# Four entry projections of the self attention moved into the end of the cross attention, with shared banks and buffers

## What is computed

```python
x = _layernorm(x + _L0_xattn_ref(x, ctx_1024, mask_BxS2_bf1, ...))   # 16 heads of 128, 8 for k and v
...
attn_out = attention(rmsnorm(hidden_states, norm1_w), wq, wk, wv, wo)  # hidden_states is that x
...
def attention(x, wq, wk, wv, wo):           # H, KV, HD = 16, 4, 128; s = 512
    q = (x @ wq).reshape(b, s, H, HD)
    k = (x @ wk).reshape(b, s, KV, HD)
    v = (x @ wv).reshape(b, s, KV, HD)
    q, k = apply_rope(q, cos, sin), apply_rope(k, cos, sin)
    # scores with a causal mask, softmax over keys, times v, then wo
```

## Time and profile before

| | us |
|---|---|
| median of 3 runs | 1418.55 |
| lowest, highest | 1417.82, 1419.85 |
| the profiled execution | 1419.94 |
| its span | 1418.1 |
| TensorE busy in the span | 1308.9 (92%) |
| VectorE, ScalarE, GpSimd busy | 1023.4, 808.4, 368.7 |
| cross attention's last turn done (XT complete) | 707.4 |
| first matmul of the self attention | 709.99 |
| first scores of the self attention | 727.69 |

### The profile page before, as it was taken

One profiled execution on the slowest core, in us unless ns is written; L12 is line 12 of the kernel. 1 busy time (PEld: TensorE's weight loads), 2 busy tenths in 40 slices (PEclk: granted clock), 3 DMA queues, 4 the chain that ended last, 5 costly groups with the idle time before them and its releaser, 6 DMA issues. The chain is left out here.

```text
span 1418.1 us, 24554 instructions
## 1 busy us (share of the span) xinstructions
PE 1308.9 (92%) x7925; PEld 711.2 (50%) x7925; DVE 1023.4 (72%) x1966; ACT 808.4 (57%) x1460; POOL 368.7 (26%) x602
## 2 busy tenths in 40 slices
PE   7988999999999999999597999999877999999994
PEld 4444444444444444444254555555434556666771
DVE  5847777777777777778668787888778564566676
ACT  5547666666666666667427565565754454455552
POOL 5402020101111110102356465563425100000025
PEclk9999999999999999999799999999988999999997
DMA  8317676667575757598284353535585766677653
GB/s 254 61 36 146 128 134 117 145 119 153 106 155 106 153 108 151 110 180 147 81 256 71 70 142 66 130 65 104 103 164 205 236 232 190 223 240 238 223 149 120
DMA packets 451868, 206.18 MB, mean 145 GB/s; under 512 B 401088, under 2 KB 415424, under 8 KB 451776
## 3 DMA queue, kind: packets, MB, share of 16 engines
q1 hardware_dynamic: 448640, 196.67, 59.2%
q0 software_dynamic: 2560, 8.39, 1.8%
q10 hardware_dynamic: 576, 0.00, 0.0%
HBM read 87.38 MB, written 16.45 MB: 73 GB/s over the span
## 5 line engine op out<-in xcount | busy, mean ns | idle before, releaser
L1546 DVE SCALAR_TENSOR_TENSOR X<-xa_SC,xa_rs,X 128x1024 f16<-128x1024 f32 x128 | 164.4, 1284 | 98.3 <-issue 97.7
L1354 ACT ACTIVATE X<-xa_SC,xa_rs 128x1024 f16<-128x1024 f32 x128 | 147.1, 1149 | 110.4 <-POOL xa_rs L1044 110.4
L1222 PE MATMUL xa_psS<-xa_KT,xa_QT 128*128 128x512 f16 x768 | 186.4, 379 | 6.0 <-DVE xa_mn L1579 4.6
L1234 PE MATMUL xa_psO<-wide,xa_V 128*128 128x512 f16 x768 | 173.5, 383 | 7.5 <-DMA wide<-X 7.5
L1044 POOL TENSOR_SCALAR xa_rs<-xa_rc,flag 128x1 f32<-128x1 f32 x128 | 33.9, 265 | 517.3 <-DVE xa_rc L1539 517.3
L1579 DVE CUSTOM_DVE_ANT_0 xa_SC<-xa_psS,maskb 128x1024 f32<-128x1024 f32 x128 | 155.1, 1212 | 4.7 <-PE xa_psS L1222 2.4
L1376 ACT ACTIVATE xa_SC<-xa_SC,xa_mn 128x1024 f32<-128x1024 f32 x128 | 145.4, 1136 | 13.7 <-DVE xa_mn L1579 13.6
L1234 PEld LDWEIGHTS xa_psO<-wide,xa_V 128*128 128x128 f16 x768 | 74.6, 99 | 102.5 <-issue 17.3
L1222 PEld LDWEIGHTS xa_psS<-xa_KT,xa_QT 128*128 128x128 f16 x768 | 73.4, 98 | 90.6 <-DVE xa_mn L1579 9.4
L1376 ACT ACTIVATE sa_SC<-sa_SC,sa_mn 128x128 f32<-128x128 f32 (+3 forms) x128 | 71.5, 558 | 72.2 <-DVE sa_mn L1579 71.8
L2072 PE MATMUL rmoe_psG<-rmoe_XGT,W 128*128 128x352 f16 (+6 forms) x768 | 108.4, 291 | 2.1 <-DVE rmoe_XGT L2180 2.1
(11 more groups left out here) (295 smaller groups left out, 2253.7 us busy)
## 6 DMA issues: line engine op xcount, KB each, us to landing
first<-in_L_ffn_w_dram SPq DMA_DIRECT2D x12, 2048.0 KB, 12.2
W2raw<-in_L_ffn_w_dram SPq DMA_DIRECT2D x8, 2048.0 KB, 9.2
expert_rows_dram<-zeros SPq DMA_DIRECT2D x10, 512.0 KB, 9.3
xa_WPraw<-in_L_xattn_Wq_dram SPq DMA_DIRECT2D x8, 512.0 KB, 4.8
xa_WOraw<-in_L_xattn_Wo_dram SPq DMA_DIRECT2D x8, 512.0 KB, 4.5
first<-in_L_ffn_wq_dram SPq DMA_DIRECT2D x4, 1024.0 KB, 7.9
first<-in_L_ffn_wo_dram SPq DMA_DIRECT2D x4, 1024.0 KB, 5.8
first<-in_L_ffn_w_dram SPq DMA_DIRECT2D x8, 512.0 KB, 4.9
```

What stands on the lines that cost most here:

```text
L1222: last = nc.tensor.matmul(psS[j % NSC][:, c:c + cw], QT[b][:, hq, g, t * P:(t + 1) * P], KT[b][:, hk, c:c + cw], start=(q == 0), stop=(q = ...
L1234: last = nc.tensor.matmul(psO[:, c:], V[b][:, hv, blk, :], PT[g % NPT][:, blk, hp, c:], start=(blk + q == 0), stop=(blk == NBLK - 1 and q ...
L1354: nc.scalar.activation(PN[j % NPN][:, 0:w // P, 0, :], by_block(SC[j % NSC], w), ACT.Identity, scale=rs[:, j % 4:j % 4 + 1]).then_inc(norm ...
L1546: nc.vector.scalar_tensor_tensor(out=PN[j % NPN][:, 0:w // P, 1, :], in0=by_block(SC[j % NSC], w), scalar=rs[:, j % 4:j % 4 + 1], in1=PN[j ...
```

## The change

- **Where the projections are made.** K, Q0, Q1 and Q2 of batch 0 are made in xa's end by a new `entry_project`, between the turns of batch 1. They need XT of batch 0 complete and the split weights. They go into the banks psO, psJ1, psJ0 and psJ2, which are free once the outputs that were in them have been added.
- **What is done with them there.** VectorE turns K and Q0 (`entry_turn`), GpSimd adds K's two products, ScalarE and GpSimd write K's halves. Q0's sum, and all of Q1 and Q2 after the matmuls, stay for sa, whose engines begin with their semaphores raised by the jobs already made (MADE = 4, TURNED = 2, ROTATED = 1). sa's TensorE begins with Q3 and V, in psO and psJ1.
- **What is shared.** The banks psO and psJ are allocated once for both calls (`banks`). KT0, V0 and the buffers rA and rB lie in the memory of the context CT, which xa no longer reads then (`carried`).
- **Order and waits.** In xa's end VectorE does tile 2's low half before the first output add of batch 1, tile 3's after tile 4's centring, and tile 5's after tile 7's. The second projection in the first head group's steps waits for one job more. The wait for the stores of X stands behind the six jobs on VectorE, not ahead of them.

```diff
 
         if isinstance(h, int) and h == 1 and k < 2:
             return k + 1
+        if causal and isinstance(h, int) and h == 0 and k == 1:
+            return 2
         return 3 if last else (3, 3, 3, 3, 3, 3, 3, 2, 4, 3)[k]
...
+        if causal:
+            KT0, V0, rA, rB = carried
+            QT = [sb(f"QT{b}", [P, 2, groups, S], F16) for b in range(B)]
+            KT = [KT0, sb("KT1", [P, 2, keys], F16)]
+            V = [V0, sb("V1", [P, 2, NBLK, HD], F16)]
+        else:
...
-        rA = [sb(f"rA{i}", [P, S if causal else 1], F32) for i in range(3)]
-        rB = [sb(f"rB{i}", [P, S if causal else 1], F32) for i in range(3)]
...
-        psO = pb("psO", [P, 512])
-        psJ = [pb(f"psJ{i}", [P, 512]) for i in range(NJ)]
-        ring = psJ
+        psO, psJ = banks
         acc = [psS[-1][:, NB * 512 - 512:NB * 512], psJ[1], psJ[0], psJ[2]]
+        entry_bank = [psO, psJ[1], psJ[0], psJ[2], psO, psJ[1]]
+        ring, RING = (entry_bank, 4) if causal else ([psJ[i % NJ] for i in range(JP)], NJ)
+        MADE, TURNED, ROTATED = (4, 2, 1) if causal else (0, 0, 0)
...
+            nK, _, nA, nB = next_carried
...
             if causal:
-                rope_sum(0, 0, 0, 0)
-                for i in range(1, JP - 1):
+                pool.sem_inc(rope_added, ROTATED)
+                pool.sem_inc(rope_done, ROTATED)
+                rope_sum(0, 0, ROTATED, ROTATED)
+                for i in range(ROTATED + 1, JP - 1):
                     rope_sum(0, 0, i, i)
...
+                pool.wait_ge(entry_turned, 1)
+                nc.gpsimd.tensor_tensor(nA[0], nA[0], nB[0], ALU.add).then_inc(entry_added, 1)
+                pool.wait_ge(entry_hi, 1)
+                nc.gpsimd.tensor_tensor(nK[:, 1, :], nA[0], nK[:, 0, :], ALU.subtract).then_inc(entry_lo, 1)
+                pool.wait_ge(entry_lo, 1)
...
                         pe.wait_ge(job_free, jobs_before(h) + t + 1)
                     last_output(t, early)
+
+            def entry_project(i):
+
+                if i == 0:
+                    pe.wait_ge(next_lo, len(next_pieces))
+                    pe.wait_ge(norm_lo, TPB)
+                else:
+                    pe.wait_ge(job_free, last_job(TPB + i) + 1)
+                for q, (hw, hx) in enumerate(PAIRS):
+                    for k in range(DC):
+                        last = nc.tensor.matmul(entry_bank[i][:, :],
+                                                next_k[:, hw, k, :] if i == 0 else next_q[:, hw, k, i - 1, :],
+                                                XT[:, hx, k, 0:S], start=(q + k == 0), stop=(q == 2 and k == DC - 1))
+                last.then_inc(entry_ready, 1)
 
...
+            if MADE:
+                pe.sem_inc(job_ready, MADE)
+            for i in range(MADE, JP):
                 if i == min(i for i, (kind, _) in enumerate(proj) if kind != "q"):
                     wait_from(pe, wp_done, WP0)
-                project(0, 0, i, i, ring[i % len(ring)], len(ring))
...
-                for i in range(TPB, NT):
-                    norm_pe(pe, i)
+                entry_project(0)
+                norm_pe(pe, 4)
+                entry_project(1)
+                norm_pe(pe, 5)
+                norm_pe(pe, 6)
+                entry_project(2)
+                norm_pe(pe, 7)
+                entry_project(3)
...
-            for i in (0, 1, 2, 3, 5, 4) if causal else range(JP):
+            if ROTATED:
+                act.sem_inc(rope_hi, ROTATED)
+            for i in (1, 2, 3, 5, 4) if causal else range(JP):
                 if plain(i):
-                    job_high(0, 0, i, i, ring[i % len(ring)])
+                    job_high(0, 0, i, i, ring[i])
                 else:
...
+                act.wait_ge(entry_added, 1)
+                nc.scalar.copy(nK[:, 0, :], nA[0]).then_inc(entry_hi, 1)
                 norm_x(7)
...
+            def entry_turn(i):
+
+                entryC, entryS = entry_rope
+                dve.wait_ge(entry_ready, i + 1)
+                nc.vector.tensor_tensor(nA[i], entry_bank[i][:, :], entryC[:], ALU.mult)
+                nc.vector.tensor_tensor(nB[i][64:128, :], entry_bank[i][0:64, :], entryS[0:64, :], ALU.mult)
+                nc.vector.tensor_tensor(nB[i][0:64, :], entry_bank[i][64:128, :], entryS[64:128, :],
+                                        ALU.mult).then_inc(entry_turned, 1)
 
...
+            if TURNED:
+                dve.sem_inc(job_free, TURNED)
+            for i in range(TURNED, JP):
+                job_low(0, 0, i, i, ring[i])
             if route is not None:
                 dve.wait_ge(kept, 16 * NT)
-            for i in range(JP):
-                job_low(0, 0, i, i, ring[i % len(ring)])
...
                 norm_dve(dve, 1)
+                norm_dve(dve, 2)
...
                 h = 2 * kv_heads - 1
                 output_add(h, 1, t, jobs_before(h) + JO + t, acc[t])
                 norm_stats(TPB + t)
-                if t > 1:
-                    norm_dve(dve, t + 2)
+                if t == 2:
+                    norm_dve(dve, 4)
                 norm_centre(TPB + t)
-                if t < 2:
-                    norm_dve(dve, t + 2)
+                if t == 0:
+                    norm_dve(dve, 3)
             if tail is not None:
+                norm_dve(dve, 5)
+                entry_turn(0)
                 norm_dve(dve, 6)
                 norm_dve(dve, 7)
+                entry_turn(1)
 
...
+        both = ExitStack()
+        CT = both.enter_context(nc.sbuf_tensor("CT", [P, 2, DCTX // P, B * S2], F16))
+        flat = CT[:].rearrange("p l k t -> p (l k t)")
+        HW = 2 * S
+        carried = (flat[:, 0:HW].rearrange("p (l t) -> p l t", l=2),
+                   flat[:, HW:2 * HW].rearrange("p (l m c) -> p l m c", l=2, c=HD),
+                   [flat[:, (2 + i) * HW:(3 + i) * HW].bitcast(F32) for i in range(3)],
+                   [flat[:, (5 + i) * HW:(6 + i) * HW].bitcast(F32) for i in range(3)])
...
+            banks = (both.enter_context(nc.psum_tensor("att_psO", [P, 512], F32)),
+                     [both.enter_context(nc.psum_tensor(f"att_psJ{i}", [P, 512], F32)) for i in range(3)])
...
-                      tail=(norm1_w, X2, (own_raw, own_split, own_in), own_loads, own_wo[:, 0, :], kept))
+                      tail=(norm1_w, X2, (own_raw, own_split, own_in), own_loads, own_wo[:, 0, :], kept,
+                            ((ropeC, ropeS), carried, 4)), banks=banks)
...
-                  route=(norm2_w, XW, XP, gate_w, lg, top, idx, next_loads, zeroed, 16 * len(cleared), kept, first))
+                  route=(norm2_w, XW, XP, gate_w, lg, top, idx, next_loads, zeroed, 16 * len(cleared), kept, first),
+                  banks=banks, carried=carried)
+        both.close()
```

More of the change, by code:

```diff
@@ L710, in attention @@
 def attention(nc, name, X, XT, KVT, identF, weights, Wq, Wk, Wv, Wo, kv_heads, groups, keys, mask_of, flag, rope, ready=False, tail=None,
-              clear=(), wo_raw=None, turned=None, route=None):
+              clear=(), wo_raw=None, turned=None, route=None, banks=None, carried=None):
     NS = groups * TPB
```

15 lines of the change are left out of this document (9 added, 6 removed).

## The result

The changed kernel took 1416.09 us (median of 20 runs, 1410.97 to 1421.03), the kernel before 1418.92 in the same series (20 runs, 1417.46 to 1427.33). The ratio is 0.9973, with an interval of 0.9962 to 0.9984: by it a gain of 3.8 us (2.3 to 5.4; the medians alone differ by 2.8), where 8.5 had been forecast, and a time of 1410.0 in a range of 1407.0 to 1414.5. The profiled execution of after took 1418.63 us, span 1416.7 (before: 1419.94, span 1418.1).

What follows compares the result with a forecast made beforehand. TensorE, busy 92%, was taken to be alone on the path in the new block's six projections. -11.4 + 2.0 + 0.5 + 0.4 = -8.5 us from the median 1418.55 gave 1410.0 us, range 1407.0 to 1414.5.

Steps and rivals of the forecast that it cites:

- Removed: 11.4: Block's start: six projections' 17.7 us before the first scores shrink to 6.3, midway between warm and cold clock; 10.4 to 12.4.
- Added to the stage's end: 2.0: Cross attention's end: with projections between the turns, the block ends at 710.6 instead of 708.6 us.
- the cold tail: Rival, chance 0.14: clock falls in the cross attention's end, K and Q0 at 1.2 GHz, 2.1 to 4.2 us more, 1412 to 1414.
- its slower case: Rival, chance 0.04: all four projections and four turns at the low clock, 10.2 us on the tail, 1420.9 us.
- Lateness at the start: 0.5: Self attention's start: VectorE does Q1's and Q2's banks first, so later jobs and the first mask come late; 0 to 0.9 us.
- DMA queue: 0.4: SyncE's queue: transposes and next weights come behind the zero-fills; no cost if cover holds, 2.5 us without; 0.4 taken.
- the collision: Rival, chance 0.2: SyncE's full queue delays the first values until tile 3 lands at 741.9 us; 1412.1 us (1411.3 to 1413).
- the cover: TensorE's 4.50 us standstill before the second values, waiting for ScalarE's eviction, was to hide the late transposes.
- the last rival: Chance 0.07: earlier scores only wait later, for weights' halves or an unseen queue; at most 2 us left, 1416.5 to 1420.
- The second rival: Chance 0.2: queue collision without cover, first values wait for tile 3, all behind moves by 6.5 us only; 1412.1 us.
- "The shift is carried to the end.": After the seam: order of work unchanged and every DMA issued by its place, so the whole -8.5 us reaches the end.
- a new wait between 765 and 1034 us: Sign, later in the self attention: a wait that before doesn't have would show the prediction wrong altogether.

Runs made afterwards that it cites:

- zeros_early: The changed kernel with the 12 zero-fills issued by SyncE in the cross attention's end, ahead of its stores of X: 1411.16 us, ratio 0.9939 to the kernel before.

## Why the prediction was wrong

Point by point, by its own steps, in the profiled execution of after (which reached the seam 0.95 + 0.99 = 1.94 us later than before for reasons ahead of it):

- **Removed: 11.4.** Measured 17.70 - 5.26 = 12.4, the upper bound of the term. The clock was up when the block began, so the middle between a warm and a cold Q3 was not needed.
- **Added to the stage's end: 2.0.** 713.60 - 709.99 - 1.94 = 1.7. The laid-out order held nearly row by row: the first projection at 697.77 - 1.94 = 695.8 (forecast 695.8), the block's first matmul at 711.7 (712.0), the first scores at 716.9 (717.3). One wait of 1.30 us between the turns, and a full clock; the cold tail and its slower case didn't come.
- **Lateness at the start: 0.5.** 0.01: zeros_early, where only this could show, loses nothing in the 16 steps.
- **DMA queue: 0.4. This is the step that failed**, and with it the 0.2 that I gave the collision. It cost 3.7 us (3.44 to 3.94). The queue itself was foreseen nearly rightly: the first values were to wait for tile 3, until 741.9, and did until 743.60 - 1.94 = 741.7. (The 5.6 us of transfer that I took for the weights stand in no row; their last piece landed at 738.6 counted like this, where I had 737.5.) What I mis-weighed is the cover. I took TensorE's wait for sa_OT (4.50 us) as the slack, and for TensorE it held: the wait shrank to 1.98. But the other user of the same landings had less: "the buffers that hold the probabilities", of which I had written that tile 1's is the nearest, and which I let count for the small term. ScalarE waited 4.07 us for that buffer and had 1.96 to hide it in. The 2.1 us left over went through to GpSimd's pieces of the weights, a chain of 12.1 us that releases the next head group's first projection without slack, in before too (1.45 us of wait). I had named these halves as well, in the last rival, and let them go with the remark that they hang on ScalarE's order, which moves along; the order does, but ScalarE's wait was new in it. The longer idle time brought the clock down at the projection, 1.4 us more, which wasn't in the term at all.

  The second rival (the wait uncovered on TensorE) gave 1412.1, nearer than my forecast, but not by the path that the rows show; with the landings as late as I had laid them out myself, it deserved more than 0.2. The Trainium skill's rule, from "DMA: Bandwidth & Descriptors", "Queues, rings and completion order", that each DMA engine takes a ring's descriptors in order, speaks for that rival. The trace agrees: the transpose issued behind 5.5 MB of zeros landed 8.5 us after its issue, in an empty queue 2.3.
- **"The shift is carried to the end."** It isn't: 2.9 us are lost at 1017 us, where neither order nor waits changed. The prediction treated the clock only at the seam, though the earlier trace rows show it falling where TensorE mostly stands still, and the last half has two such places. I had no term for it, and only "a new wait between 765 and 1034 us" as a sign. There was no new wait, so that sign would have missed it.

With the terms measured, the sum is -12.4 + 1.7 + 0.0 + 3.5 + 2.9 = -4.3 us in that execution. Without the last two, -10.7: what zeros_early shows (-10.96 and -10.62 at the seam), and about 9 us by its medians. So the idea of the change was right, and better than forecast; it fell short because of what it ran into.

## What to carry to other kernels

When a change brings work forward, list every DMA that comes forward with it and what is queued ahead of it then; here moving 12 transfers that nobody was waiting for was worth about 5 us, more than the change had brought. A wait that shrinks is cover for one engine only: for a transfer that lands late, list every engine that waits for it, also the one that waits to write its source buffer anew, set each wait against the idle time of that engine right behind it, and follow what is left over to the next place at which one engine releases another without slack. And where the clock gate falls at idle stretches, look at which work stands behind each of them: moving a whole stage, with nothing in it changed, can put the fall from harmless work onto the path.

## What the hardware showed that I had not expected

- A full queue holds up the issuing engine as well: the weights' three issues took 1.32 to 1.66 us each on SyncE in after, a transpose 2.15, against 0.50 to 0.56 and 1.24 in zeros_early.
- The same two idle stretches (3.2 and 2.8 us) with 3.6 us of matmuls between them saw no fall of the clock in before, one in the first in zeros_early, and one in the second in the five profiled executions of after. The Trainium skill, "TensorE: Matmul & The Clock Gate", section "HAM oscillation", describes bursts between DMA waits of some 3 to 5 us, each of which starts cold. Here, with waits of 3.2 and 2.8 us, one of the two bursts started cold or none, and the price was 0 to 2.9 us for the same work.
- A fall need not cost: two bursts at 1.2 GHz in zeros_early ended inside idle time that was there anyway (6.46 against 6.44 us from the values to the output).
